# Graph attention and gated graph layers on one core: weights on ScalarE's queue, x in halves, e_j by ones, and a few steps of the steady loop in another order

## The reference

```python
h = jnp.maximum(_layernorm(x, axis=-1), 0.0)
x = x + _L0_gnn_ref(h, adj, L0_gnn_W, L0_gnn_a)
h = jnp.maximum(_layernorm(x, axis=-1), 0.0)
x = x + _L1_gnn_ref(h, adj, ...)

# _L0_gnn_ref
Wh = h @ W
e_i, e_j = Wh @ a[:F, 0], Wh @ a[F:, 0]
e = e_i[:, :, None] + e_j[:, None, :]
e = jnp.where(e > 0, e, 0.2 * e)
e = jnp.where(adj > 0, e, -9e15)
return jax.nn.elu(jax.nn.softmax(e, axis=2) @ Wh)

# _L1_gnn_ref: A = (adj != 0)
for i in range(3):
    m = h @ weight[i]
    aggr = einsum('bst,bsd->btd', A, m)
    h = gru_cell(aggr, h, w_ih, w_hh, b_ih, b_hh)
```

## Time and profile before

| | us |
|---|---|
| median of 3 runs (lowest, highest) | 708.62 (707.83, 711.08) |
| the profiled execution | 710.96 |
| its span in the profile | 709.2 |
| busy: PE, DVE, ACT, POOL | 633.1, 529.7, 455.3, 290.6 |

### The profile page before, as it was taken

One profiled execution on the slowest core, in us unless ns is written; L12 is line 12 of the kernel. 1 busy time (PEld: TensorE's weight loads), 2 busy tenths in 40 slices (PEclk: granted clock), 3 DMA queues, 4 the chain that ended last, 5 costly groups with the idle time before them and its releaser, 6 DMA issues.

```text
span 709.2 us, 8823 instructions
## 1 busy us (share of the span) xinstructions
PE 633.1 (89%) x2845; PEld 469.6 (66%) x2845; DVE 529.7 (75%) x1218; ACT 455.3 (64%) x777; POOL 290.6 (41%) x295
## 2 busy tenths in 40 slices
PE   2686999979999899979999799997999799997996
PEld 2465767667676776657676576766766686765774
DVE  5767988589875997669885798759976788655444
ACT  2884786558865688557865588646885577553443
POOL 1203544167144452455441671445523534415442
PEclk9799899999999899999999999999999899999998
DMA  6521220122301231004301223012310030001001
GB/s 217 176 90 60 90 89 31 61 60 91 118 0 61 89 119 60 30 31 133 105 31 59 61 90 119 1 60 87 122 60 30 32 111 36 1 1 30 1 1 30
DMA packets 28670, 47.40 MB, mean 67 GB/s; under 512 B 1672, under 2 KB 19408, under 8 KB 28624
## 3 DMA queue, kind: packets, MB, share of 16 engines
q1 hardware_dynamic: 28624, 46.84, 20.2%
HBM read 42.60 MB, written 4.23 MB: 66 GB/s over the span
## 4 chain that ended last, share of the span: by engine, by line
PE 56%; DVE 20%; ACT 9%; POOL 7%; issue 5%; DMA 3%; SPq 0%; DVEq 0%; ACTq 0%; POOLq 0%
PE ps_x L928 14%; PE ps_g L966 13%; PE ps_x L909 7%; DMA x_nat<-in_x 3%; POOL rstd L273 3%; DVE score L659 2%; DVE hkT L737 2%; ACT score L386 2%; DVE nn L734 2%; PE ps_x L949 2%; PE ps_z L975 2%; PE ps_r L976 2%; PE ps_r L975 2%; PE ps_z L977 2%; PE ps_z L976 2%
## 5 line engine op out<-in xcount | busy, mean ns | idle before, releaser
L966 PE MATMUL ps_g<-edges,h_hi 128*128 128x512 f32 x384 | 163.8, 426 | 8.0 <-DVE h_lo L743 6.6
L966 PE MATMUL ps_g<-edges,h_lo 128*128 128x512 f32 x384 | 157.6, 410 | 0.0
L295 POOL TENSOR_SCALAR tz<-tz 128x512 f32<-128x512 f32 x48 | 34.3, 716 | 252.3 <-ACT tz L427 252.3
L928 PE MATMUL ps_x<-probT,h_nat 128*128 128x512 f32 x224 | 98.9, 594 | 0.0
L966 PEld LDWEIGHTS ps_g<-edges,h_hi 128*128 128x128 f32 x384 | 77.2, 201 | 27.7 <-DVE h_lo L743 10.3
L659 DVE CUSTOM_DVE_ANT_0 score<-score,away 128x1024 f32<-128x1024 f32 x64 | 88.5, 1383 | 7.4 <-ACT score L380 6.5
L386 ACT ACTIVATE score<-score,nmax 128x1024 f32<-128x1024 f32 x64 | 73.7, 1151 | 31.4 <-DVE nmax L659 30.5
L966 PEld LDWEIGHTS ps_g<-edges,h_lo 128*128 128x128 f32 x384 | 76.8, 200 | 15.1
L393 ACT ACTIVATE probT<-ps_x 128x512 f32<-128x512 f32 x128 | 71.0, 597 | 17.1 <-PE ps_x L909 17.0
L909 PE MATMUL ps_x<-ident,score 128*128 128x128 f32 x512 | 70.9, 280 | 11.5 <-ACT score L386 10.2
L909 PEld LDWEIGHTS ps_x<-ident,score 128*128 128x128 f32 x512 | 59.6, 144 | 26.3 <-ACT score L386 16.8
(11 more groups left out here) (133 smaller groups left out, 1341.9 us busy)
## 6 DMA issues: line engine op xcount, KB each, us to landing
adj_in<-in_adj SPq DMA_DIRECT2D x64, 512.0 KB, 3.3
x_nat<-in_x SPq DMA_DIRECT2D x8, 512.0 KB, 4.5
ej<-ej_kept_at SPq DMA_DIRECT2D x8, 512.0 KB, 3.5
out<-nn SPq DMA_DIRECT2D x16, 256.0 KB, 2.3
probT<-in_L_gnn_weight SPq DMA_DIRECT2D x1, 192.0 KB
probT<-in_L_gnn_w_ih SPq DMA_DIRECT2D x1, 192.0 KB
probT<-in_L_gnn_w_hh SPq DMA_DIRECT2D x1, 192.0 KB
ej_kept_at<-ej_row SPq DMA_DIRECT2D x8, 4.0 KB
```

The costliest lines, as they stand in the source:

```text
L928: last = pe.matmul(bank_of("agg", c, par)[:], h_nat[par][:, j, :], probT[:, j, :], start=(j == 0), stop=(j == T - 1))
L966: last = pe.matmul(ps_g[c][:], part[:, s, :], edges[par][:, s, cols(c)], start=(s == 0 and part is h_hi), stop=(s == T - 1 and part is h_lo))
```

## The change

First stage. The seven weight transfers leave SP's queue for ACT's, the four that are needed first ahead; x of graph 0 comes in two halves with a semaphore each, its normalisation goes by halves, and x of graph 1 is loaded after two tiles of `adj`. For graph 0 the trip of e_j through DRAM goes: DVE multiplies the identity by each tile's column (`first_diag`), PE multiplies a matrix of ones by that (`first_wide`, 128x512 in fp32, one per half), and ACT copies the two results straight into `ej`. Each half of a transposed tile has a bank of its own, and from tile 2 on DVE copies the lower half (`first_probT`) and ACT the upper one alone. `setup_gates` moves behind the first score, `setup_layers` behind the second transposed tile, the edges of tiles 4 to 7 behind the loop, and `norm1(1)` and `h_tiles(1)` behind it too. Half 0 of the attention is finished within the loop.

Steady loop. SP loads x of graph b+3 in body b ahead of the stores (`load_x`). POOL does `z_times_h(b, 2, 1)` ahead of the second `rstd2_half`; ACT does `n_gate(b, 2, 1)` and `leaky_tile(b+2, 0)` ahead of `h0_half(a, 1)`; PE does `neighbours(a, 0, 0, 1)` ahead of `h0T_half(a, 1)`.

```diff
@@ sync
-            sp.dma_start(x_nat[0][:], x_v[0]).then_inc(x_loaded, 16)
-            for dst, src in weights:
-                sp.dma_start(dst, src).then_inc(w_loaded, 16)
-            sp.wait_ge(x_loaded, 16)
+            for c in range(2):
+                sp.dma_start(x_nat[0][:, c * TH:(c + 1) * TH, :], x_v[0][:, c * TH:(c + 1) * TH, :]).then_inc(x0_loaded[c], 16)
+            for t in range(2):
+                sp.dma_start(adj_in[t][:], adj_v[0, t]).then_inc(adj_loaded[t], 16)
+            for c in range(2):
+                sp.wait_ge(x0_loaded[c], 16)
             sp.dma_start(x_nat[1][:], x_v[1]).then_inc(x_loaded, 16)
...
-            spread_ej(0, 0, True)
...
             spread_ej(1, 1)
+            def load_x(b):
+                sp.wait_ge(x1_done, b * 2 - 2)
+                sp.wait_ge(x_loaded, b * 16 - 16)
+                sp.dma_start(x_nat[b % 2][:], x_v[b]).then_inc(x_loaded, 16)
+            load_x(2)
             def body(b, par, attend, prepare):
-                if prepare:
-                    sp.wait_ge(x1_done, b * 2 + 2)
-                    sp.wait_ge(x_loaded, b * 16 + 32)
-                    sp.dma_start(x_nat[par][:], x_v[b + 2]).then_inc(x_loaded, 16)
...
+                if b + 3 < B:
+                    load_x(b + 3)
                 for c in range(2):
                     sp.wait_ge(out_done, b * 2 + c + 2)
@@ gpsimd, body
                 z_times_h(b, L - 1, 0)
+                z_times_h(b, L - 1, 1)
                 if attend:
                     rstd2_half(b + 1, 1)
-                z_times_h(b, L - 1, 1)
@@ scalar, first
+                load_weights()
                 h_tiles(0, 0, 0)
                 h_tiles(0, 0, 1)
-                row_of_ej(0, 0)
+                first_ej_half(0)
+                first_ej_half(1)
...
-                        probT_tile(0, 0, t - 1)
+                        probT_tile(0, 0, t - 1, [0] if t >= 3 else [0, 1])
+                    if t == T - 1:
+                        elu_exp(0, 0)
                     exp_tile(0, t)
-                    if t == 2:
-                        h_tiles(1, 1, 0)
-                        h_tiles(1, 1, 1)
-                    if t == TH + 2:
+                    if t == TH + 1:
                         aggT_half(0, 0, 0, True)
...
+                probT_tile(0, 0, T - 1, [0])
+                h0_half(0, 0, 0)
+                aggT_half(0, 0, 1, True)
+                h_tiles(1, 1, 0)
+                elu_exp(0, 1)
+                h_tiles(1, 1, 1)
+                h0T_half(0, 0, 0)
+                h0_half(0, 0, 1)
                 row_of_ej(1, 1)
+                h0T_half(0, 0, 1)
                 leaky_tile(1, 1, 0)
@@ scalar, body
                 z_gate(b, 2, 1)
-                if attend:
-                    h0_half(a, a_par, 1)
                 n_gate(b, 2, 1)
                 if prepare:
                     leaky_tile(b + 2, par, 0)
                 if attend:
+                    h0_half(a, a_par, 1)
                     h0T_half(a, a_par, 1)
@@ vector, new functions
+            def first_diag(c):
+                dve.wait_ge(first_ej, c + 1)
+                dve.wait_ge(const_done, 2)
+                col = ej_col[:, c * TH:(c + 1) * TH].rearrange("p (t o) -> p t o", o=1)
+                dve.tensor_tensor(diag[c][:], ident[:].rearrange("p (o j) -> p o j", o=1).broadcast_to([P, TH, P]),
+                                  col.broadcast_to([P, TH, P]), ALU.mult).then_inc(diag_done, 1)
+            def first_probT(t):
+                dve.wait_ge(probT_ps, 2 * t + 2)
+                dve.tensor_copy(probT[:, TH:T, tile_cols(t % TH)],
+                                bank_of("probT", 2 * t + 1, 0, True)[:].rearrange("p (j i) -> p j i", j=TH)
+                                ).then_inc(probT_dve, 1)
@@ vector, first
                 for t in range(T):
                     scores(0, t)
+                    if t >= 3:
+                        first_probT(t - 1)
                     if t + 1 < T:
                         away_tile(0, 0, t + 1)
-                        edge_tile(0, 0, t + 1)
+                    if t < TA:
+                        edge_tile(0, 0, t)
+                    if t == 0:
+                        setup_gates()
+                    if t == TH + 2:
+                        att_half(0, 0, 0, True)
+                x1_sum(0, 0, 0)
+                first_probT(T - 1)
+                norm2(0, 0, 0)
+                norm1(1, 1)
@@ tensor
+            def first_wide(c):
+                pe.wait_ge(diag_done, c + 1)
+                pe.matmul(ps_x[c][:], ones[:], diag[c][:].rearrange("p t j -> p (t j)"), start=True, stop=True
+                          ).then_inc(wide_ps, 1)
...
                 for t in range(T):
                     probT_tile(0, 0, t)
-                    if t == TH + 2:
+                    if t == 1:
+                        setup_layers()
+                    if t == TH + 1:
                         att_half(0, 0, 0, True)
-                    if t >= 2:
-                        first_agg_pair(t // 2 * 2 - 2, t % 2)
+                    if 2 <= t and t % 2 == 0:
+                        first_agg_pair(t - 2, 0)
+                        first_agg_pair(t - 2, 1)
...
                 if attend:
+                    neighbours(a, a_par, 0, 0, 1)
                     h0T_half(a, a_par, 1)
-                    neighbours(a, a_par, 0, 0, 1)
```

More of the change, by code:

```diff
@@ L51, in gat_gru_kernel @@
         minus_half = sb("minus_half", [T])
+        ones = sb("ones", [P])
         w0 = sb("w0", [F])
@@ L120, in gat_gru_kernel @@
         ps_t = [ps_hn, ps_r]
-        w_loaded, x_loaded = sem("w_loaded"), sem("x_loaded")
+        x0_loaded = [sem(f"x0_loaded{c}") for c in range(2)]
+        w0_loaded, w_loaded, x_loaded = sem("w0_loaded"), sem("w_loaded"), sem("x_loaded")
         adj_loaded = [sem(f"adj_loaded{t}") for t in range(TA)]
@@ L176, in bank_of, with prob_count, ln_count @@
                 return FIRST_BANK[kind, k]
+            if first and kind == "probT":
+                return ps_x[k % 2]
             n = JOB[kind, k]
             return ps_x[(n + par + JOBS[n][5]) % 2]
+        def prob_count(b, t, k):
+            if b == 0 and t >= 2:
+                return (probT_dve, t - 1) if k == 1 else (probT_done, t + 3)
+            return probT_done, 2 * (b * T + t) + k + 1 - (T - 2 if b > 0 else 0)
+        def ln_count(b):
+            return b + 2 if b > 0 else 2
         def adj_count(b, t):
@@ L218, in load_adj, with spread_ej @@
                 sp.dma_start(adj_in[t % TA][:], adj_v[b, t]).then_inc(adj_loaded[t % TA], 16)
[L220 removed]
+            def spread_ej(b, par):
                 sp.wait_ge(row_done, b + 1)
@@ L261, in _ @@
             pool.memset(minus_half[:], -0.5)
+            pool.memset(ones[:], 1.0)
             pool.memset(ident[:], 0.0).then_inc(const_done, 1)
@@ L900, in bank_free @@
                     if not isinstance(m, int) or -ahead <= m < B - ahead and not (m == 0 and (job, k) in FIRST_BANK):
-                        pe.wait_ge(s, (m + ahead) * per + count)
+                        if job == "probT" and m == 0:
+                            for half in range(2):
+                                pe.wait_ge(*prob_count(0, T - 1, half))
+                        elif job == "probT":
+                            pe.wait_ge(*prob_count(m, k // 2, k % 2))
+                        else:
+                            pe.wait_ge(s, (m + ahead) * per + count)
                         return
@@ L934, in first_agg_pair @@
                 i = slice(t % TH * P, (t % TH + 2) * P)
-                pe.wait_ge(probT_done, 2 * (t + 2))
+                for half in range(2):
+                    pe.wait_ge(*prob_count(0, t + 1, half))
                 if t == 0:
-                    pe.wait_ge(setup_dve, 7)
+                    pe.wait_ge(setup_dve, 8)
                 for j in range(k * TH, (k + 1) * TH):
```

198 lines of the change are left out of this document (115 added, 83 removed).

## The result

| | before | after |
|---|---|---|
| median, us (lowest, highest; runs) | 709.19 (707.83, 711.08; 4) | 696.69 (696.38, 697.30; 4) |
| the profiled execution, its span | 710.96, 709.2 | 696.65, 694.8 |
| busy: PE, DVE, ACT, POOL | 633.1, 529.7, 455.3, 290.6 | 623.7, 526.0, 451.7, 282.5 |

The change makes the kernel 1.8% faster: the ratio is 0.9823, with a 95% interval of 0.9809 to 0.9837. The two spans differ by 14.4 us, the medians by 12.5, since the profiled execution of before was one of its longer ones.

A forecast was written before the change was run, and what follows sets the result against it. DVE's readiness at the start of a body, not PE's gap alone, was taken to bound the kernel; 1.2 + 1.6 + 1.2 + 3.0 = 7.0 us off the median of 708.62 gave 701.6, range 695 to 709.

The forecast's parts named there:

- the forecast's own 698 to 705: Whole kernel: the time range belonging to the forecast of 701.6 us itself, given a chance of 0.5.
- bodies 1 to 5 gain 1.6: Steady loop: DVE passes its second score near 324.0 and x waits of 2.9 us go; bounds loss 1.9, gain 5.7.
- The hold behind the new root: End of a body: DVE's split held until POOL's first half is done at 317.1, ending at 318.25; second hold on scores.
- Body 6: No first normalisation on DVE, so PE leads; its `probT` comes at 323.6, a gain of 1.2 us (0.2 to 1.6).
- Body 7: No attention, PE alone; first 8 of 24 products done inside the old gap, a gain of 3.0 us (1.5 to 3.6).
- The first stage: Start of the kernel up to body 0's first `g_lo`: a gain of 1.2 us, bounds 4.3 and a loss of 1.5.
- (a): PE's gap counts in full: neighbours end 2.8 us earlier in each of seven bodies, time 688; chance 0.06.
- `probT` over 2 us earlier: On PE: `probT` of a body moving by over 2 us in every body would show the forecast wrong.
- (b): First stage: the e_j trip through DRAM is hidden by overlap, the stage keeps 4.3 us, time 698.5; chance 0.16.
- (c): End of a body: POOL's root behind the product delays h, split and scores; 3.5 us slower, 712.1; chance 0.09.
- (d): DVE's holds eat early x; only the last two bodies and part of the first stage gain, 705 to 708.6; chance 0.19.

The follow-up runs named there:

- new orders alone: The kernel before with the three orders of POOL, ACT and PE, x loaded where it was: median 702.32 us, ratio 0.9897 to before.
- early x: The kernel before with x of graph b+3 loaded in body b ahead of the stores, nothing else: median 707.53 us, ratio 0.9968 to before.

## Why the prediction was right or wrong

**Right:** faster by over 0.5%, within the range; 701.6 was 4.9 us too high, and the time lies outside the forecast's own 698 to 705. Misses of both signs make up the 4.9: in the traces bodies 1 to 7 gave 8.5 us more than forecast and the first stage with body 0 gave 1.2 less, and the profiled run of before was 2.3 us longer than the median from which the forecast is counted. Of the places by which a reader could check it, these held. DVE's wait for x is gone but for the first load. The gap ahead of `h_back` is 1.52, and the clock stays up behind it. The root ends at 311.35, which is 314.71 when z of the two bodies is laid on one another (3.36 later), predicted 314.8; h is there at 313.04, or 316.40, predicted 316.5. The product with ones took 2.07 and 1.91 us (1.99 was taken), and the first score came at 15.64 for 15.0. Two did not hold: the first stage's last aggregate ends at 53.91, for 52.3, and body 0's first score starts at 71.92, for 69.95.

**Wrong: the step "Against its own time of 324.55 this turn gains about 0.5 ... bodies 1 to 5 gain 1.6"**, and with it its bound of 5.7. The traces give 7.8. Three things were mis-sized. The first two are read in this table, the third in it and in the rows of POOL and DVE above (us behind the split's start; DVE's column is the start of `g_lo` plus 0.71, the distance at which PE follows it in the changed kernel):

| body | before: PE's first product of g | before: DVE would have let it start | DVE's wait for x in that | after: PE's first product of g |
|---|---|---|---|---|
| 1 | 11.05 | 10.72 | 0.26 | 9.72 |
| 2 | 12.37 | 11.14 | 0.71 | 9.73 |
| 3 | 11.13 | 10.80 | 0.80 | 9.73 |
| 4 | 11.15 | 11.08 | 0.97 | 9.70 |
| 5 | 10.89 | 10.60 | 0.16 | 9.71 |

- *The base was not the last runner.* The prediction saw that both runners lie within half a microsecond, and then counted DVE's gain alone. PE was the later in all five bodies of before, by 0.07 to 1.23: 2.3 us in sum. The 1.23 are body 2, where the clock came back late. Its rows, PE's without a bracket:

```profile
243.61 1.26 DVE L718 TENSOR_TENSOR g_lo<-ps_g,g_hi 128x512 fp32r<-128x512 f32 x2
...
245.55 0.39 PE L975 MATMUL ps_r<-g_hi,cT_hi 128*128 128x512 f32 x1
```

- *One body stood for five.* Less its wait for x, DVE let g start at 10.00 in body 3, but at 10.46, 10.43, 10.11 and 10.44 in bodies 1, 2, 4 and 5, where the first score took 1.65 us (1.32 in body 4), against 1.22 in body 3: 1.4 us in sum.
- *The hold behind the new root was priced too high.* It was to cost 0.25 us a body; instead DVE's path without x became 0.22 shorter (9.29 to 9.02 up to `g_lo`, and 0.05 back over the rest of the body): 2.4 us in five bodies. POOL's root took 2.18 in place of the 2.5 taken, `hT_lo` 1.29 in place of 1.6; DVE stood idle for h then (2.14 in the rows). POOL was through at 313.30, just after the split had begun, which was stretched to 0.52 and no more. On the prediction's clock the split was over at 317.67, for 318.25, and the second score at 323.28, for 324.0.

1.6 and these 6.1 make 7.7. The third alone would have left the gain at 4.0, within the bound; the first two took it past.

**Body 6** gave 3.27 for 1.2 by the same two errors: it is the other body of before in which the clock came back late (PE's first product of g at 12.27 us, 9.32 now), and body 3's rows were used for it. **Body 7**: 3.3 for 3.0; undoing any one of the three orders takes 2.7 to 2.9 of it back, so the mechanism named (PE's products inside the old gap) needs all three. **The first stage**: nothing for 1.2, within its bounds; in the profiled execution e_j was copied 0.8 later than taken (65.99 for 65.2), and its trip took 5.93 for the 4.76 taken, 1.2 more.

**The rivals.** (a) took the clock for everything. The signal set for it, `probT` over 2 us earlier, showed in part: it moved by 1.6 to 3.1 us against the split. But the price is refuted. With the clock at 1.00 in every window the changed kernel gained 14.3 us in bodies 1 to 7, not 19.6: in bodies 1 to 5 PE then waits some 1.05 us for the score and 0.2 for `g_lo`. The new orders alone, with the same clock, gained 1.6 in bodies 1 to 5. (DVE was not "without a pause up to 326.79", as the prediction has it: the 0.80 us for x lie in that stretch, and with the new orders alone that wait grew.) The page "TensorE: Matmul & The Clock Gate" of the Trainium skill, section "HAM oscillation — how this bites in real kernels", says that waits between groups of products put the engine back to half its clock, and advises to keep it fed. These traces agree on the fall: 0.53 behind the gap of 4.01 us, 1.00 behind that of 1.52. In bodies 1 to 5 a clock that stays up paid little until DVE no longer waited for x. (b) e_j's trip was not hidden. (c) did not come: the root ended at 314.71 on its clock, short of the 315.8 from which nothing would have been left. Without ACT's move POOL's order does cost 14 us against before, but by another path than (c)'s: n stands behind the half. (d) fell with the loop's gain.

## What to carry to other kernels

Where two engines reach a meeting point within half a microsecond of each other, take the time of the later one as the base, in every turn of the loop, and ask what both together give: removing either wait alone was worth at most 1.7 us in five bodies here, removing both 8. Read the same row in all bodies before multiplying one by five, and when a step is moved, look in every queue for what waits for it and stands ahead of something else.

## What was not expected of the hardware

After the same gap of 4.01 us PE's clock came back at different times: the mean over 8 us was 0.79 to 0.81 in four bodies of before and 0.61 and 0.63 in two; in the kernel with early x it was body 5 that had 0.61. Single microseconds of bodies 1 and 2 of before:

```profile
154.18:155.18 1.00, 1.00 (x6) 0.83 (x5) 1.00 (x3) 0.28 (x1) 0.97 (x1) 1.00 0.70 185
...
237.68:238.68 1.00, 1.00 (x4) 0.80 (x3) 1.00 (x3) 0.95 (x1) 1.00 (x1) 0.50 0.98 256
```

In body 1 the clock is at 1.00 3.5 us behind the split, in body 2 still at 0.50 after 4.5 to 5.5. With two gaps of 1.5 us it fell in five bodies of seven, and with one of 2.8 (POOL's order undone) in two of seven. What decides it is open: nothing here varied it alone. What a late clock costs can be read between bodies of one kernel: with early x alone body 5 took 83.53 us and bodies 1 to 4 82.08 to 82.28; with POOL's order undone body 5 (0.62) took 82.71 and bodies 1 to 4 81.84 to 81.88.
